# Recurrence halves of the first three head groups split and set between the score maxima

## The reference

```python
scores = jnp.einsum('bhqd,bhkd->bhqk', q, k) / jnp.sqrt(jnp.float32(D))
attn = jax.nn.softmax(scores, axis=-1)
std = jnp.einsum('bhqk,bhkd->bhqd', attn, v)
...
def step(state, xs):
    d_t, B_t, C_t, u_t = xs
    dA = jnp.exp(d_t[..., None] * A)
    state = state * dA + (d_t * u_t)[..., None] * B_t[:, None, :]
    y_t = jnp.einsum('ben,bn->be', state, C_t)
    return (state, y_t)
```

## Time and profile before

| | us |
|---|---|
| median of 3 runs | 1462.55 |
| lowest, highest | 1458.94, 1462.65 |
| the profiled execution | 1458.29 |
| its span, first to last instruction | 1456.5 |

### The profile page before, as it was taken

How to read it: one execution, slowest core, us unless ns; L and a number is a source line. 1 busy time by engine, 2 the same in 40 slices (tenths; PEclk the granted TensorE clock), 3 DMA queues, 4 the chain that set the end, 5 groups by cost and what they waited for, 6 DMA issues and landing times.

```text
span 1456.5 us, 14224 instructions
## 1 busy us (share of the span) xinstructions
PE 1211.8 (83%) x4698; PEld 558.9 (38%) x4698; DVE 1204.7 (83%) x1457; ACT 764.0 (52%) x1118; POOL 164.9 (11%) x211
## 2 busy tenths in 40 slices
PE   5563885788689989889899898889799898877996
PEld 3332422233245543333345533333355433323553
DVE  5878898989979998879889997889799998786223
ACT  6865543535367753537477653545677545352331
POOL 1000111001101120100101121001111211001001
PEclk8765796878979999789899997899799997788998
...
GB/s 193 288 162 116 172 255 165 102 145 145 58 89 248 251 133 266 127 132 87 67 135 272 164 225 194 90 164 51 89 230 259 119 256 133 146 95 15 66 101 44
DMA packets 112666, 220.20 MB, mean 151 GB/s; under 512 B 14560, under 2 KB 25312, under 8 KB 112592
## 3 DMA queue, kind: packets, MB, share of 16 engines
...
...
## 4 chain that ended last, share of the span: by engine, by line
PE 38%; DVE 38%; issue 9%; ACT 4%; DVEq 0%; ACTq 0%; POOL 0%; POOLq 0%
DVE ST L904 14%; PE ps L1381 6%; DVE ST L896 5%; PE ps L1514 5%; PE ps L1303 5%; DVE MX L960 5%; PE ps L1320 4%; PE ps L1458 3%; PE ps L1378 3%; PE ps L1474 3%; PE ps L1413 2%; DVE QAK L1131 2%; DVE QS L1118 2%; DVE ST L907 1%; PE ps L1286 1%
## 5 line engine op out<-in xcount | busy, mean ns | idle before, releaser
L904 DVE TENSOR_TENSOR_SCAN ST<-dA,ST 128x1024 f32<-128x1024 f32 x128 | 292.9, 2289 | 12.9 <-ACT dA L593 10.2
L1514 PE MATMUL ps<-V,GU 128*128 128x512 f16 x1024 | 238.0, 387 | 5.6 <-DVE V L1105 5.6
L960 DVE TENSOR_REDUCE MX<-ps 128x1 f32<-128x512 f32 x256 | 165.2, 686 | 72.8 <-PE ps L1303 72.3
L509 POOL DMA_DIRECT2D YA<-ST x128 | 109.3, 854 | 975.6 <-DVE ST L907 923.8
L593 ACT ACTIVATE dA<-DL,Aneg 128x511 f32<-128x511 f32 x256 | 168.3, 713 | 60.6 <-DVE ST L904 56.4
L731 ACT ACTIVATE PT<-ps 128x1024 f32<-128x1024 f32 x128 | 126.8, 1021 | 135.7 <-PE ps L1413 135.0
L1303 PE MATMUL ps<-KS,QS 96*128 96x512 f32 x256 | 127.4, 562 | 50.1 <-DVE MX L960 37.1
L907 DVE TENSOR_TENSOR ST<-ST,BC 128x1024 f32<-128x1024 f32 x128 | 156.8, 1225 | 4.4
L896 DVE TENSOR_TENSOR ST<-DU,BC 128x1024 f32<-128x1024 f32 x128 | 155.9, 1218 | 0.1
L1514 PEld LDWEIGHTS ps<-V,GU 128*128 128x128 bf16 x1024 | 97.0, 99 | 140.6 <-issue 30.5
L1474 PE MATMUL ps<-QS 128*128 128x512 f32 x512 | 142.9, 422 | 2.5 <-DVE QS L1118 1.6
...
## 6 DMA issues: line engine op xcount, KB each, us to landing
YA<-ST POOLq DMA_DIRECT2D x128, 512.0 KB, 7.2
...
```

What stands on the lines that cost most here:

```text
L904: nc.vector.tensor_tensor_scan(flat, dA[:, a, :, :].rearrange("p e s -> p (e s)"), flat, 0.0, ALU.mult, ALU.add).then_inc(s_scan, 1)
L960: nc.vector.tensor_reduce(MX[:, j % 2, qt, h:h + 1], ps[:, n % 2, :], AX_X, ALU.max).then_inc(s_mx, 1)
L1514: last = mm(ps[:, f % F_RING, :], GU[:, t % GU_RING, k, m * P:(m + 1) * P], XHL[:, z, k, :], start=(k == 0 and z == 0), stop=(k == KT - 1 ...
```

## The change

The maxima, the half operations and every other instruction stay the same in number and form; their place in the order of DVE and of ACT changes, in head groups 0, 1 and 2 of each batch. PE, POOL and SyncE issue the same instructions in the same order.

- `scan_half` is split into `half_input` (multiply by the B row), `half_scan` (the scan) and `half_output` (multiply by the C row); called as a whole it issues the same as before.
- Group 0: input and scan of its first half go before maximum 4, the output behind maximum 7; `splat_affinities` behind maximum 11, and `splat_weights` behind the last maximum. The other halves follow.
- Groups 1 and 2: the first half's input comes behind the first four maxima (and, in group 1, the normalise), its scan two maxima later and its output two maxima after that; the second half's input goes between maxima 11 and 12. Its scan and output, and further halves, follow the last maximum.
- ACT: `slot_halves` gives the first half to slot 0 (group 0) or 1 (groups 1 and 2), so its two exponentials come before the group-0 bias row, or behind the exponentials of slot 0. The others stay in slot 3. In batch 0 the lists of groups 1 and 2 had a half in slot 1 before.
- Group 3 (`NG - 1`) keeps its loop.

```diff
@@ -277,8 +277,7 @@
             if j == NG:
                 return [mine]
             if j < NG - 1:
-                third = len(mine) // 3
-                return [[], mine[:third], [], mine[third:]]
+                return [mine[:1], [], [], mine[1:]] if j == 0 else [[], mine[:1], [], mine[1:]]
             return [[], mine[:2], mine[2:3], mine[3:]]
 
 
@@ -694,6 +693,8 @@
                     for place in DECAYS_AT[2 * KT + u]:
                         for n, a in fill_halves(place, first):
                             exp_dA(b, n, a)
+                for n, a in slot_halves(0, first)[0]:
+                    exp_dA(b, n, a)
                 bias_row(b, 0)
                 for z in range(2):
 
@@ -711,7 +712,7 @@
                         act.wait_ge(s_kat, b + 1)
                         nc.scalar.copy(QAK[:, 2, :], ps[:, 1, :]).then_inc(s_ka, 1)
                     for kt in range(KT):
-                        if j < NG - 1 or kt != 1:
+                        if (j, kt) not in ((0, 0), (NG - 1, 1)):
                             for n, a in halves[kt]:
                                 exp_dA(b, n, a)
                         if j + 1 < NG and kt == KT - 1:
@@ -885,7 +886,7 @@
 
         @block.vector
         def _(dve):
-            def scan_half(bb, n, a, between=None):
+            def half_input(bb, n, a):
 
                 g = half(bb, n, a)
                 dve.wait_ge(s_du, bb + 1)
@@ -895,16 +896,27 @@
                     dve.wait_ge(s_yacc[a_before], 16 * (n_before + 1))
                 nc.vector.tensor_tensor(ST[:, ring(bb, n, a), :, :], DU[:, 2 * a:2 * a + 2, :],
                                         BC[:, n % BC_RING, 0:1, :].broadcast_to((P, 2, S)), ALU.mult).then_inc(s_dBu, 1)
-                if between:
-                    between()
+
+            def half_scan(bb, n, a):
+                g = half(bb, n, a)
                 dve.wait_ge(s_dBu, g + 1)
                 st = ST[:, ring(bb, n, a), :, :]
                 flat = st.rearrange("p e s -> p (e s)")
                 dve.wait_ge(s_dA, g + 1)
                 nc.vector.tensor_tensor_scan(flat, dA[:, a, :, :].rearrange("p e s -> p (e s)"), flat, 0.0,
                                              ALU.mult, ALU.add).then_inc(s_scan, 1)
-                dve.wait_ge(s_scan, g + 1)
+
+            def half_output(bb, n, a):
+                st = ST[:, ring(bb, n, a), :, :]
+                dve.wait_ge(s_scan, half(bb, n, a) + 1)
                 nc.vector.tensor_tensor(st, st, BC[:, n % BC_RING, 1:2, :].broadcast_to((P, 2, S)), ALU.mult).then_inc(s_prod, 1)
+
+            def scan_half(bb, n, a, between=None):
+                half_input(bb, n, a)
+                if between:
+                    between()
+                half_scan(bb, n, a)
+                half_output(bb, n, a)
 
             def conv(bb, e):
                 for k in range(DC - 2, -1, -1):
@@ -1044,19 +1056,44 @@
                     fill_half(2 * KT + u)
                     low_part(u)
                 max_tiles(b, 1, 0, X_AHEAD)
-                for j in range(NG):
+                for j in range(NG - 1):
+                    halves = slot_halves(j, first)
+                    x = X_CHUNK[j]
+                    if j == 0:
+                        half_input(b, *halves[0][0])
+                        half_scan(b, *halves[0][0])
+                        max_tiles(b, 1, x[0], x[1])
+                        half_output(b, *halves[0][0])
+                        max_tiles(b, 1, x[1], x[2] - 2)
+                        splat_affinities(b)
+                        max_tiles(b, 1, x[2] - 2, x[3])
+                        splat_weights(b)
+                        rest = halves[KT - 1]
+                    else:
+                        if j == KV_GROUP:
+                            normalise(b, j - 1)
+                            splat_kv(b)
+                        max_tiles(b, j + 1, x[0], x[1])
+                        if j != KV_GROUP:
+                            normalise(b, j - 1)
+                        half_input(b, *halves[1][0])
+                        max_tiles(b, j + 1, x[1], x[1] + 2)
+                        half_scan(b, *halves[1][0])
+                        max_tiles(b, j + 1, x[1] + 2, x[1] + 4)
+                        half_output(b, *halves[1][0])
+                        max_tiles(b, j + 1, x[1] + 4, x[2] + 2)
+                        half_input(b, *halves[KT - 1][0])
+                        max_tiles(b, j + 1, x[2] + 2, x[3])
+                        half_scan(b, *halves[KT - 1][0])
+                        half_output(b, *halves[KT - 1][0])
+                        rest = halves[KT - 1][1:]
+                    for n, a in rest:
+                        scan_half(b, n, a)
+                for j in (NG - 1,):
                     halves = slot_halves(j, first)
                     for c in range(KT):
-                        if j == KV_GROUP and c == 0:
+                        if c == 0:
                             normalise(b, j - 1)
-                            splat_kv(b)
-                        if j + 1 < NG:
-                            max_tiles(b, j + 1, X_CHUNK[j][c], X_CHUNK[j][c + 1])
-                        if j > 0 and j != KV_GROUP and c == 0:
-                            normalise(b, j - 1)
-                        if j == 0 and c == 1:
-                            splat_affinities(b)
-                            splat_weights(b)
                         if j == NG - 1:
                             if c == 0:
                                 splat_normalise(b)
```

## The result

| | before | changed |
|---|---|---|
| median, us | 1462.2 | 1476.41 |
| lowest, highest | 1458.94, 1462.65 | 1472.99, 1485.25 |
| ratio of the two, 95% interval | | 1.0115 [1.0084, 1.0147] |
| profiled execution | 1458.29 | 1477.84 |
| its mean granted TensorE clock | 0.872 | 0.86 |

The change makes the kernel slower: the medians are 14.2 us apart (1.0%), and the ratio over all runs is 1.0115. "Before" and "after" are from here on the kernel before and the changed kernel.

What follows compares the result with a forecast made beforehand. PE and DVE, each busy 83%, hand work to each other: PE bounds the stretch of maxima, DVE the tail of recurrence halves. Three batches at +4.65 us (+14.0) and batch 0 at -3.7 gave +10.3, 1472.8 us; range 1454 to 1483.

Steps and rivals of the forecast that it cites:

- the likeliest case: Whole kernel with PE's clock as now: +10.3 us, 1472.8, own range +4.4 to +17; chance 0.50.
- the fourth case: PE at its low clock everywhere while the maxima run: +20.6 us, 1483.1; chance 0.08.
- group 0, stretch and tail: Maxima and following recurrence halves of head group 0, batches 1 to 3: +0.2 us, bounds -1.9 and +2.
- stretch 1: Run of 16 maxima of head group 1, with DVE pieces moved in, batches 1 to 3: +2.9 us.
- tail 1: Recurrence halves behind group 1's maxima, batches 1 to 3: at most 0.85 us comes back before PE is late.
- stretch 2: Run of 16 maxima of head group 2, with DVE pieces moved in, batches 1 to 3: +2.5 us.
- tail 2: Recurrence halves behind group 2's maxima, batches 1 to 3: only 0.1 us comes back, since DVE then needs ACT's exponential.
- batch 0: Its head groups, where one half already stands whole among the maxima: -3.7 us, bounds -6.8 and -1.2.
- The walk at the low level: Groups 1 and 2 stepped through with PE at 1.2 GHz: DVE waits 1.8 and 1.3 us; +4.0 us each.
- ACT at nothing: Moving one exponential pair per group ahead costs nothing, since ACT idles 8.44 us before the group-0 bias row.
- DVE's idle at the maxima: DVE's waiting at the maxima, 72 us in the whole kernel, falls by 20 to 30 us.
- The filled-idle rival: Each DVE piece runs while PE makes the next products, so no maximum waits: -8.8 us, 1453.8; chance 0.15.

Runs made afterwards that it cites:

- row_load_first: The changed kernel with SyncE's B and C row loads of batch 0, group 1 issued ahead of head group 3's loads; 1476.6 us, ratio 1.0115.
- the doubled products: Each product for the maxima computed twice into the same bank: on the kernel before 1476.02 us (+16.3), on the changed kernel 1483.93 (+24.2 against before).
- group0_only: The changed kernel with DVE's order of groups 1 and 2 as before; 1465.53 us, +5.1 against the kernel before, ratio 1.0038.
- act_order_only: The kernel before with only ACT's order changed, DVE's order as before; 1461.06 us, +0.7, ratio 1.0008.
- pieces_at_values: The changed kernel with groups 1 and 2's first half behind maxima 7, 9, 13, second half whole afterwards, DVE's group 0 old; 1456.57 us, -3.2 against before.
- inputs_early: The kernel before with the first multiply after groups 0 and 1 moved behind maximum 11 and 7, batches 1 to 3; 1454.15 us, -6.2, ratio 0.9944.
- combined: The kernel before with early multiplies in batches 1 to 3 and batch 0's half cut at PE's value products, groups 1 and 2; 1446.17 us, -15.2.
- one_half_early: The changed kernel with DVE's group 0 old and groups 1 and 2's second-half multiply back behind the maxima; 1477.4 us, +16.0 against before, ratio 1.0109.

## Why the prediction was right, and where not

The sign and the range held: +14.2 us against +10.3, in the likeliest case's own range of +4.4 to +17. The mechanism did too: the tails had almost nothing to give, and the stretches grew. That the number came so near is in part luck. The profiled pair, from which the steps can be read, is 19.55 us apart, next to the fourth case (+20.6), and its head groups cost twice what was forecast. By steps, mean of batches 1 to 3 in the profiled pair:

| step | forecast | measured |
|---|---|---|
| group 0, stretch and tail | +0.2 | +1.8 |
| stretch 1 | +2.9 | +3.0 |
| tail 1 | -0.85 | -0.65 |
| stretch 2 | +2.5 | +3.8 |
| tail 2 | -0.1 | -0.3 |
| sum of a batch | +4.65 | +7.6 |
| batch 0 | -3.7 | -2.3 |
| head groups of all four batches | +10.3 | +20.5 |

**Tails.** Right for batches 1 to 3: no tail gave more than 0.94 us, for 3.5 us taken out behind group 0 and 5.9 behind groups 1 and 2. One bound was read from batch 1 and did not hold for batch 3. There DVE took ACT's exponential 1.02 us after it was ready, and not 0.1:

```profile
1290.43 0.63 ACT L744 ACTIVATE X<-X 128x512 f32<-128x512 f32 x1
...
1292.08 0.74 DVE L1000 SCALAR_TENSOR_TENSOR X<-ps,par,X 128x512 f32<-128x512 f32 x1
```

and it is this tail 2 that gave the 0.94. In batch 0 tail 2 got 2.46 us shorter, more than the 1.6 that the prediction named as the sign of being wrong. It gave 1.35 in `row_load_first`, where the wait for a row ahead of it is gone; the forecast for this tail was 1.2. In batch 1 the time taken out turned into DVE waiting, 4.04 and 3.85 us at the normalise behind groups 1 and 2, 3 to 5 forecast, and then for ACT's exponential, 1.92 (it was ready 0.1 us ahead before). DVE of after:

```profile
644.42 0.69 DVE L978 TENSOR_TENSOR X<-ps,RD 128x512 f32<-128x512 f32 x1 [4.04 <-ACT RD L662]
...
675.28 0.69 DVE L978 TENSOR_TENSOR X<-ps,RD 128x512 f32<-128x512 f32 x1 [3.85 <-ACT RD L662]
...
679.28 0.75 DVE L1012 SCALAR_TENSOR_TENSOR X<-ps,par,X 128x512 f32<-128x512 f32 x1 [1.92 <-ACT X L745]
```

**Stretches 1 and 2.** The walk at the low level named the waits themselves: 1.8 us ahead of maximum 10 and 1.3 ahead of maximum 14. Measured are 2.00 and 1.15, both in group 2 of every batch and in group 1 of batch 1; in group 1 of batches 2 and 3 only the first came, and the stretch took 19.5 instead of 20.7 us. What failed in size is the way I mixed the two walks. I took over the shares of low clock that the old stretches show, 60% and 46%, and weighted the walks with them. In group 1 this came out (+2.9, measured +3.0). In group 2 all three stretches ran as long as the low walk has it (18.96, 18.66 and 18.66 against 19.0), and in batches 2 and 3 with a clock mean of 0.73, low for 54% of the time, which by my formula gives +2.7 and not +3.7. Batch 2 of after shows why:

```profile
966.80:976.00 9.20, 6.25 (x25) 2.58 (x28) 9.19 (x11) 2.05 (x2) 0.00 (x0) 0.91 0.58 185
976.00:984.50 8.50, 8.50 (x26) 3.18 (x25) 5.35 (x9) 3.26 (x4) 0.85 (x1) 0.50 0.33 64
```

The clock was high while DVE did its pieces and PE waited for them, and low from the second value block to the last pair, where PE sets the pace. A share of the stretch says nothing of which products it covers. The sentence that PE "has risen after such phases so far", which stood against the fourth case, was the weak one: by the profiled pair a batch costs 7.6 us, the size of that case (7.25), though part of it is group 0.

The rule quoted with the prediction from the Trainium skill ("Perfetto Trace Analysis", Matmul Optimizations), that power follows use and matmuls should stand back to back, would have given the low walk more weight. The trace agrees in part: the doubled products brought the clock of stretch 2 from 0.77 to 1.00, but in `group0_only` it stayed at 0.50 for 13.0 us in which PE was busy for 12.96.

**Group 0.** Forecast +0.2 with a bound of +2; measured +1.8. Two things were left out. The first is the moved multiply itself, 1.22 us in the rows of before. In batches 1 to 3 it took 2.01, 2.23 and 2.21. Batch 1, POOL and DVE:

```profile
587.88 2.50 POOL L524 TENSOR_TENSOR X<-X 128x512 f32<-128x512 f32 x2 [22.28 <-ACT X L705]
```

```profile
589.45 2.01 DVE L897 TENSOR_TENSOR ST<-DU,BC 128x1024 f32<-128x1024 f32 x1
```

The change put it where POOL subtracts two 128 x 512 tiles (line 524), and the multiply ended 1.08 us behind POOL's end (590.38), as if it could hardly begin before. Over all runs, ten multiplies of a half took longer than 1.23 us, 1.93 to 2.31. They are those that began while such a subtraction ran, 0.8 us or more before its end, and each ended 1.08 or 1.09 us behind it. In batch 0, where POOL was done, the multiply took 1.22. This puts 0.8 to 1.0 us at the head of stretch 0. In `group0_only` the three multiplies are together 3.2 us too long, and that kernel costs 5.1 us in all. What they are worth in the end is not shown, since no run moves them alone.

The second is the clock. The walk had PE at its low level only up to the first value block. In fact that block and the second took 1.94 and 1.93 us, and DVE waited 2.32 us for the last pair, for which it had not waited before:

```profile
606.08 1.29 DVE L972 TENSOR_REDUCE MX<-ps 128x1 f32<-128x512 f32 x2 [2.32 <-PE ps L1340]
```

And PE, ahead of it:

```profile
594.42 1.39 PE L1340 MATMUL ps<-KS,QS 96*128 96x512 f32 x2 [2.54 <-DVE MX L972]
...
599.66 1.94 PE L1357 MATMUL ps<-PT,V 128*32 128x512 f32 x8
...
602.68 1.93 PE L1357 MATMUL ps<-PT,ones 128*32 128x512 f32 x8
```

The transposes started 19.0 us behind the start of the stretch (608.52 - 589.5), forecast 16.7.

**Batch 0.** Stretch 1 fell by 1.4 (forecast 1.2). The exponential of the fourth half ended 1.2 us sooner against the last maximum, as forecast (333.35 - 329.62 against 333.66 - 328.7). But "no start of a half waits for one", said of the accumulating DMAs, left out the other DMA that a half waits for, its rows. With the 2.48 us wait, stretch 2 grew by 2.2 where -1.3 was forecast; without it, in `row_load_first`, it fell by only 0.3, since it too ran as the low walk has it (18.67 against 19.0).

**ACT at nothing.** Right: +0.7 us within [-2.5, +4.7] by `act_order_only`, and the bias row of group 0 did not start later behind the transposes in batch 1 (0.63 us behind their start, before 0.98).

**DVE's idle at the maxima.** Forecast to fall by 20 to 30 us, fell by 8.7. It is the same miss: the pieces filled idle early in the stretch, and PE's slower work opened as much behind them. `pieces_at_values` had the expected fall (23.9 us), which shows that this idle is no measure of the gain.

**The filled-idle rival** is the case that a rule of the Trainium skill picks ("Perfetto Trace Analysis", Optimizing Scalar/DVE Operations), that breaking up instructions which cause bubbles elsewhere may let work finish sooner. The runs agree only for the right places: cut and placed beside the value blocks 3.2 us faster, cut and placed early 16.0 slower, uncut 21.0 slower.

**What stays open.** What brings PE's clock down was not shown. Early waits and a longer low phase come together in every early-piece order, but not everywhere: in stretch 2 of `pieces_at_values`, batch 1, PE waited 1.67 us for DVE ahead of products 12 and 13 and stayed at 1.00, and stretch 2 of the old order began with the same two waits (0.84 and 0.55 us) in `inputs_early`, batch 2, and in `combined`, batch 1, and took 12.6 us in the one and 15.3 in the other. Nor does PE's being busy bring it up at once: in `one_half_early` PE was busy without a break from 627.0 to 637.3 us, and the level was low all the same:

```profile
627.00:637.30 10.30, 10.30 (x36) 3.77 (x35) 6.11 (x10) 3.26 (x4) 0.87 (x1) 0.54 0.27 51
```
